# Head convolution of a decoder: symmetric pairs, their causal convolution and the sum over them, redistributed over four engines

## Reference, cut to what matters

```
kv = jnp.einsum('bhil,bhjl->bijhl', k_, v_)
kv_f = jnp.fft.rfft(kv, n=fft_size)
kernel_f = jnp.fft.rfft(ssm_kernel, n=fft_size)
y = jnp.fft.irfft(kv_f * kernel_f, n=fft_size)[..., :L]
out = y + kv * D[None, None, None, :, None]
out = jnp.einsum('bijhl,bhil->bjhl', out, q_)
```

## Time and profile before

| | us |
|---|---|
| median of 3 runs (1696.04 to 1698.32) | 1698.15 |
| the profiled execution: its own time | 1701.08 |
| its span in the trace | 1699.4 |
| PE / DVE / ACT / POOL busy | 1492.0 / 1142.3 / 672.0 / 712.8 |

### The profile page before, as it was taken

How to read it: one execution, slowest core, us unless ns; L and a number is a source line. 1 busy time by engine, 2 the same in 40 slices (tenths; PEclk the granted TensorE clock), 3 DMA queues, 4 the chain that set the end, 5 groups by cost and what they waited for, 6 DMA issues and landing times. The chain is left out here.

```text
span 1699.4 us, 34312 instructions
## 1 busy us (share of the span) xinstructions
PE 1492.0 (88%) x8665; PEld 1189.4 (70%) x8666; DVE 1142.3 (67%) x3594; ACT 672.0 (40%) x1818; POOL 712.8 (42%) x1162
## 2 busy tenths in 40 slices
PE   5899999999999999779897899876761999999997
PEld 4788888888888888566665666656760776677765
DVE  4777777777777777669999999997654223223232
ACT  3777777777767777610000100001331223332232
POOL 2011111111111110158887288861767355545553
PEclk9999999999999999999999899995555999999999
DMA  5544434343434343641113011104896455555552
GB/s 163 130 109 108 101 98 101 90 108 87 107 82 103 90 105 88 233 154 49 43 49 137 17 46 49 43 18 155 191 248 131 80 102 95 97 99 100 99 100 47
DMA packets 89774, 172.21 MB, mean 101 GB/s; under 512 B 26384, under 2 KB 26384, under 8 KB 88656
## 3 DMA queue, kind: packets, MB, share of 16 engines
q1 hardware_dynamic: 63584, 122.46, 27.3%
q0 software_dynamic: 18176, 35.80, 11.8%
q10 hardware_dynamic: 7920, 12.93, 3.0%
HBM read 78.10 MB, written 44.79 MB: 72 GB/s over the span
## 5 line engine op out<-in xcount | busy, mean ns | idle before, releaser
L1097 PE MATMUL ps_y<-pairs,taps 128*128 128x288 f32 x1280 | 324.5, 410 | 35.4 <-DVE prods L1170 32.1
L1097 PEld LDWEIGHTS ps_y<-pairs,taps 128*128 128x128 f32 x1280 | 238.6, 190 | 120.8 <-POOL pairs L1041 41.6
L853 ACT ACTIVATE probs<-neg_scores,neg_max 128x256 f32<-128x256 f32 x512 | 255.2, 505 | 25.9 <-DVE neg_max L654 25.9
L1170 DVE TENSOR_TENSOR prods<-ps_y,q_g 128x224 f32<-128x224 f32 (+7 forms) x960 | 251.4, 404 | 17.7 <-issue 8.0
L654 DVE CUSTOM_DVE_ANT_0 neg_scores<-ps_scores,alibi 128x256 f32<-128x256 f32 x512 | 194.9, 418 | 90.4 <-PE ps_scores L519 61.9
L1041 POOL TENSOR_TENSOR pairs<-ctx_g 128x32 f32 (+11 forms) x512 | 215.7, 459 | 42.4 <-PE ps_y L1097 32.0
L1533 POOL DMA_INDIRECT out<-y_row,back x72 | 113.2, 1572 | 174.9 <-DMA out<-y_row,back 140.6
L863 ACT ACTIVATE probs_t<-ps_probs_t 128x512 f32<-128x512 f32 x208 | 124.0, 596 | 130.4 <-PE ps_probs_t L530 130.4
L530 PE MATMUL ps_probs_t<-ident,probs 128*128 128x128 f32 x1024 | 159.3, 280 | 8.7 <-ACT probs L853 8.7
L403 POOL COPY inv_wide<-inv_sum 128x512 f32<-128x512 f32 x32 | 20.6, 672 | 318.7 <-DVE inv_sum L670 318.7
L1920 DVE TENSOR_TENSOR st_lo<-ps_x,st_hi 128x512 fp32r<-128x512 f32 x72 | 49.8, 692 | 145.8 <-ACT st_hi L1711 145.8
(11 more groups left out here) (190 smaller groups left out, 3232.6 us busy)
## 6 DMA issues: line engine op xcount, KB each, us to landing
q_stack<-q_hi SPq DMA_DIRECT2D x128, 128.0 KB, 2.3
k_stack<-k_hi SPq DMA_DIRECT2D x128, 128.0 KB, 2.3
taps<-kernel_pad SPq DMA_DIRECT2D x64, 256.0 KB, 3.1
x_in<-in_x SPq DMA_DIRECT2D x16, 512.0 KB, 3.6
q_stack<-q_lo SPq DMA_DIRECT2D x64, 128.0 KB, 2.3
k_stack<-k_lo SPq DMA_DIRECT2D x64, 128.0 KB, 2.3
x_rows<-x_mid SPq DMA_DIRECT2D x16, 512.0 KB, 3.0
ctx_g<-in_ctx_t SPq DMA_DIRECT2D x2, 4096.0 KB, 12.2
```

What stands on the lines that cost most here:

```text
L853: last = act.activation(probs[h % 2][:, tt, :], neg_scores[h % 2][:, tt, :], ACT.Exp, bias=neg_max[par][:, h, tt:tt + 1], scale=-1.0, accu ...
L1097: last = pe.matmul(ps_y[par][:, lc, 0:GB * PAIRS], taps[r][:, block_cols:block_cols + P], pairs[par][:, mc, :, :], start=(mc == 0), stop=( ...
L1170: last = dve.tensor_tensor(prods[par][:, :, :, to:to + n, term], y[:, :, :, col:col + n], head_of(q_g, own, q_from, n), ALU.mult)
```

## The change

- ACT gets work: for each head it copies q (`turn_q`) and ctx (`turn_ctx`) twice in a row into rings of 16 (`q_ring`, `ctx_ring`), so that a row of 8 read from element e on is the cyclic turn by e. It also copies y out of PSUM (`keep_y`, three instructions) into rows of 11 (`y_rows`), laid out so that each of the 8 terms is a plain row of 8.
- `form_pairs` is two multiplications in place of eight: one of 1024 elements (own channels repeated, times the ring) and one of 128. `pairs` has four buffers, and the pairs are formed three heads ahead.
- `multiply` is four multiplications in place of fifteen: one of 32 x 5 x 8 = 1280 elements and three of 256. It reads `y_rows` and `q_ring`, both in SBUF, and writes `prods` with the channel innermost. The elements are 2048, as before.
- The eight terms are summed by `halve` (1024 elements) and `quarter` (512) on DVE and `fold` (256) on POOL, which writes `q_g` and counts `z_ready`. The reduction is gone.
- PE waits for `y_kept` of the head two before, no longer for `prods_ready`, and writes each batch's 36 columns 64 apart in PSUM.
- Queues: DVE multiply(h), quarter(h-1), halve(h). POOL fold(h-1), form_pairs(h+3). ACT turn_q(h), keep_y(h), turn_ctx(h+3). The loops are unrolled by four heads.

```diff
-                    pool.wait_ge(y_ready, k * 2 + (g * SH + par + 1 - 2 + Y_START))
-                    for col, i, j, n in pair_segments():
-                        last = pool.tensor_tensor(pairs[par][:, :, :, col:col + n], ...)
-                    first = prods[par][:, :, :, :, 0:FOLD]
-                    pool.tensor_tensor(first, first, prods[par][:, :, :, :, SD - FOLD:SD], ALU.add).then_inc(folded, 1)
+                def form_pairs(g, k, r):
+                    h = k * PAIR_BUFS + (g * SH + r)
+                    pool.wait_ge(y_ready, h + (1 - PAIR_BUFS + Y_START))
+                    wait_apart(pool, ctx_ring_ready, h + 1, passed)
+                    own = by_lane(ctx_g, k * PAIR_BUFS + r)
+                    to = pairs[r][:, :, :, :].rearrange("p m b q -> p (m b) q")
+                    pool.tensor_tensor(to[:, :, 0:HALF * SD].rearrange("p n (d i) -> p n d i", i=SD),
+                                       own.unsqueeze(2).to_broadcast([P, EC * GB, HALF, SD]),
+                                       turned(ctx_ring[r % 2], HALF), ALU.mult)
+                    pool.tensor_tensor(to[:, :, HALF * SD:PAIRS], own[:, :, 0:HALF], own[:, :, HALF:SD], ALU.mult)\
+                        .then_inc(pairs_ready, 1)
+                def fold(g, k, r):
+                    wait_apart(pool, quartered, k * PAIR_BUFS + (g * SH + r + 1), passed)
+                    pool.tensor_tensor(by_lane(q_g, k * PAIR_BUFS + r), prods[r % 2][:, :, 0, :], prods[r % 2][:, :, 1, :],
+                                       ALU.add).then_inc(z_ready, 1)
...
-                    pe.wait_ge(prods_ready, h + (1 - 2 + PRODS_START))
+                    pe.wait_ge(y_kept, h + (1 - 2 + KEPT_START))
...
+                def turn_ctx(g, k, r):
+                    if not (is_int(k, 0) and r < 2 and g == 0):
+                        act.wait_ge(pairs_ready, k * PAIR_BUFS + (g * SH + r - 1))
+                    ring_of(ctx_ring[r % 2], ctx_g, k * PAIR_BUFS + r).then_inc(ctx_ring_ready, 1)
+                def turn_q(g, k, r):
+                    act.wait_ge(prods_ready, k * PAIR_BUFS + (r + g * SH + 1 - 2 + PRODS_START))
+                    ring_of(q_ring[r % 2], q_g, k * PAIR_BUFS + r)
+                def keep_y(g, k, r):
+                    act.wait_ge(y_ready, k * PAIR_BUFS + (r + g * SH + 1 + Y_START))
+                    ...
+                    act.activation(whole_rows[:, :, :, 0:SD], near, ACT.Copy)
+                    act.activation(whole_rows[:, :, 0:HALF - 1, SD:ROW], near[:, :, 1:HALF, SD - HALF + 1:SD], ACT.Copy)
+                    act.activation(rows[:, :, HALF * ROW:ROWS].rearrange("p n (u i) -> p n u i", u=2), ..., ACT.Copy).then_inc(y_kept, 1)
...
-                        for to, q_from, term in uses:
-                            last = dve.tensor_tensor(prods[par][:, :, :, to:to + n, term], y[:, :, :, col:col + n],
-                                                     head_of(q_g, own, q_from, n), ALU.mult)
-                    dve.tensor_reduce(head_of(q_g, k * 2 + par, 0, SD), prods[par][:, :, :, :, 0:SD - FOLD], AX_X,
-                                      ALU.add).then_inc(z_ready, 1)
+                    dve.wait_ge(y_kept, h + (1 + KEPT_START))
+                    dve.wait_ge(z_ready, h + (1 - 2 + Z_START))
+                    to, rows, q = prods[r % 2], y_rows[r % 2], q_ring[r % 2]
+                    dve.tensor_tensor(to[:, :, 0:HALF + 1, :], main_rows(rows, HALF + 1), turned(q, HALF + 1), ALU.mult)
+                    for e in range(HALF + 1, SD):
+                        first = (SD - e) * (ROW - 1)
+                        last = dve.tensor_tensor(to[:, :, e, :], rows[:, :, first:first + SD], q[:, :, e:e + SD], ALU.mult)
+                    last.then_inc(prods_ready, 1)
+                def halve(g, k, r):
+                    wait_apart(dve, prods_ready, k * PAIR_BUFS + (r + g * SH + 1 + PRODS_START), passed)
+                    dve.tensor_tensor(to[:, :, 0:4, :], to[:, :, 0:4, :], to[:, :, 4:8, :], ALU.add).then_inc(halved, 1)
+                def quarter(g, k, r):
+                    wait_apart(dve, halved, k * PAIR_BUFS + (r + g * SH + 1), passed)
+                    dve.tensor_tensor(to[:, :, 0:2, :], to[:, :, 0:2, :], to[:, :, 2:4, :], ALU.add).then_inc(quartered, 1)
```

More of the change, by code:

```diff
@@ L961, in build_decoder @@
         TAP_BUFS = 4
[L962 to L969, removed]
+        PAIR_BUFS = 4
+        PAIRS_AHEAD = 3
+        HALF = SD // 2
+        ROW = SD + HALF - 1
+        ROWS = HALF * ROW + SD
         with ExitStack() as scope:
@@ L980, in build_decoder @@
             taps = [sb(f"taps{i}", [P, E]) for i in range(TAP_BUFS)]
-            pairs = [sb(f"pairs{i}", [P, EC, GB, PAIRS]) for i in range(2)]
-            prods = [sb(f"prods{i}", [P, EC, GB, SD, SD]) for i in range(2)]
+            pairs = [sb(f"pairs{i}", [P, EC, GB, PAIRS]) for i in range(PAIR_BUFS)]
+            prods = [sb(f"prods{i}", [P, EC * GB, SD, SD]) for i in range(2)]
+            y_rows = [sb(f"y_rows{i}", [P, EC * GB, ROWS]) for i in range(2)]
+            q_ring = [sb(f"q_ring{i}", [P, EC * GB, 2 * SD]) for i in range(2)]
+            ctx_ring = [sb(f"ctx_ring{i}", [P, EC * GB, 2 * SD]) for i in range(2)]
             xn_g = [sb(f"xn_g{i}", [P, TT, E]) for i in range(2)]
@@ L1013, in head_of, with by_lane, turned, main_rows @@
                 return v.rearrange("p m b s i -> p m b (s i)")
+            def by_lane(tile, h):
+                v = tile[:, :, :].rearrange("p m (b s i) -> p (m b) s i", b=GB, s=SH)[:, :, ds(h, 1), :]
+                return v.rearrange("p n s i -> p n (s i)")
+            def turned(tile, n):
+                return bass.AP(tensor=tile, offset=0, ap=[[EC * GB * 2 * SD, P], [2 * SD, EC * GB], [1, n], [1, SD]])
+            def main_rows(tile, n):
+                return bass.AP(tensor=tile, offset=0, ap=[[EC * GB * ROWS, P], [ROWS, EC * GB], [ROW, n], [1, SD]])
+            def quads(eng, emit):
+                for r in range(PAIR_BUFS):
+                    emit(0, r)
+                with eng.Fori(1, QUADS - 1) as k:
+                    for r in range(PAIR_BUFS):
+                        emit(k, r)
+                for r in range(PAIR_BUFS):
+                    emit(QUADS - 1, r)
+            def head_at(k, r, ahead=0):
+                return k + (r + ahead) // PAIR_BUFS, (r + ahead) % PAIR_BUFS
+            def is_int(k, value):
+                return isinstance(k, int) and k == value
             skewed = bass.AP(tensor=kernel_pad, offset=1, ap=[[P + E, SH], [1, P], [1, E]])
@@ L1059, in _ @@
                                         newton[:, GT:NT], c_rstd_step, 0, c_rstd, passed)
[L1060 to L1065, removed]
+                    quads(pool, lambda k, r: head_step(g, k, r))
+                    fold(g, QUADS - 1, PAIR_BUFS - 1)
                 pool.wait_ge(x2_moments, GT)
@@ new lines, in quarter, with head_step @@
+                def quarter(g, k, r):
+                    wait_apart(dve, halved, k * PAIR_BUFS + (r + g * SH + 1), passed)
+                    to = prods[r % 2]
+                    dve.tensor_tensor(to[:, :, 0:2, :], to[:, :, 0:2, :], to[:, :, 2:4, :], ALU.add).then_inc(quartered, 1)
+                def head_step(g, k, r):
+                    multiply(g, k, r)
+                    if not (is_int(k, 0) and r == 0):
+                        quarter(g, *head_at(k, r, -1))
+                    halve(g, k, r)
@@ L1197, in _ @@
                     dve.wait_ge(c_xt_kept, (g + 1) * GB + XT_START)
[L1198 to L1206, removed]
+                    quads(dve, lambda k, r: head_step(g, k, r))
+                    quarter(g, QUADS - 1, PAIR_BUFS - 1)
                     for t in range(GT):
```

69 lines of the change are left out of this document (41 added, 28 removed).

## The result

The changed kernel takes 1786.68 us (median of 4 runs, 1783.06 to 1791.85), the kernel before 1698.24 beside it: a ratio of 1.0526, 95% interval 1.0496 to 1.0556. It is 88 us slower. Forecast were 1727 us and a range up to 1785, so the direction held, the forecast size was a third of the true one, and the time lies just outside the range.

The account below looks back on a forecast made before the run. DVE was taken to bound the kernel before; afterwards DVE and POOL times add. Group 0 +14.4, group 1 +13.3 and normalising +1 made +28.7 on 1701.08, 1729.8, set to 1727 us as that execution lay 2.9 above median; range 1700 to 1785.

Parts of the forecast that it names:

- DVE sets the pace before, PE next: Heads of the kernel before: DVE never stops at 5.64 us a head; PE needs 5.09 and waits 0.55.
- DVE and POOL shut each other out, so their times add: Changed heads: two-SBUF-input DVE instructions and POOL's SBUF reads exclude each other, so 3.74 + 2.41 = 6.15 us a head.
- I take 1.67 (same operation, tile and rows of eight): POOL's 1024-element pairs product: 1.67 us, from 1.375 ns an element in smaller products; 2.36 kept as upper end.
- second rival: Heads: exclusion plus dearer instructions, such as POOL's large product at 2.36 us, adding 40 us; 1745 to 1790 us, chance 28%.
- DVE alone 3.74: DVE's six instructions a head: 4.64 us at the plain rate, less 0.15 hidden for each, gives 3.74 instead of 5.64.
- the spread write alone made an element cost 1.9 ns: DVE's fifteen old multiplications: 1.9 ns an element against plain 1.057, the difference laid to writing eight words apart.
- the 0.25 us a head set beside the sum for rows that start on an odd word: DVE's new multiplications: odd-starting rows of eight at 1.30 ns an element would add 0.25 us a head, some 16 us.
- 0.1 us a head for handing over: Heads: waits between DVE and POOL where neither is ready, estimated at 0.1 us a head, between none and 0.3.
- The first rows of POOL beside the normalising, 1 us: Ahead of group 0: DVE's normalising beside POOL's first, longer pairs instructions adds 1 us (0 to 2).
- The first rival, PE sets the pace: Heads: no exclusion, PE at 4.97 us a head sets the pace; 43.5 us saved, 1655 us, chance 10%.
- The third rival: DVE's rows of eight stay at 1.9 ns an element, 1922 us; a lower TensorE clock shares its 5% chance.
- ACT's copies and PSUM columns 64 apart cost nothing: Heads: ACT's 3.0 us lies under PE's 5.09, only 1.8 us a group in the chain; spaced columns cost PE nothing.

Follow-up runs that it names:

- Pairs ahead: The kernel before with only pairs in four buffers, formed three heads ahead: 1700.61 us against 1700.02, ratio 1.0006.
- pool_writes_only: The changed kernel with POOL's 1024-element product replaced by writes of constants, so part of the computation is missing: 1665.9 us against 1692.45 for the kernel before.
- y_from_psum: The changed kernel with y multiplied straight from PSUM in nine instructions, without ACT's copies of y: 1672.15 us, ratio 0.988 to the kernel before.
- pool_probe: The changed kernel with six more POOL instructions of various sizes, operations and rows behind the last fold: 1787.41 us against 1692.45 for the kernel before.
- after_eight_products: The changed kernel with pairs formed by the eight short products of the kernel before: 1783.7 us against 1695.23 for the kernel before.
- psum_four_prods: The changed kernel with y multiplied from PSUM in nine instructions, no y copies, and four prods buffers instead of two: 1650.16 us, ratio 0.9724 to the kernel before.

## Why the prediction was right on the sign and wrong on the size

*DVE sets the pace before, PE next*: held. Pairs ahead, which touch neither, changed nothing.

*DVE and POOL shut each other out, so their times add*: held, and it makes the loss of the heads: with POOL's large product or DVE's multiplication taken out of it, the same kernel is faster than the one before. Shown from POOL's side by pool_writes_only and from DVE's by y_from_psum. The head of 7.18 us is the sum of what each holds, 4.03 + 3.14.

*The step that failed* is "I take 1.67 (same operation, tile and rows of eight)" for POOL's large product. It measured 2.29, with 2.25 between ends where the prediction's sum had 1.52. The other row of its size, 2364 ns, was a subtraction in one run and was set aside as another operation; pool_probe shows that size decides and operation and rows don't. The forecast had this case in its second rival (1745 to 1790, 28%), where the result fell, and the range ended 2 us short of it. The mechanism was right; this term of the sum was mis-sized. The term: 58 heads x 0.73 = 42 us.

*DVE alone 3.74*: it measured 4.03. The large multiplication came in as forecast (1.50 and 1.35 between ends). But what an instruction hides behind the one before, taken as 0.15 from the short ones, was 0.08 for `quarter` (0.68 long, 0.60 between ends) and `halve` (1.21 and 1.13), and the three short ones took 0.95 in place of 0.79. The term: 64 x 0.29 = 19 us. That the spread write alone made an element cost 1.9 ns was wrong as a reason: it was 0.8 of the 3.92 us. The rate taken for the new rows was right, and the 0.25 us a head set beside the sum for rows that start on an odd word did not come (1280 elements in 1.49 us).

*0.1 us a head for handing over*: there was none; -6 us.

*The first rows of POOL beside the normalising, 1 us*: it was 5.1. In the changed kernel the first product of PE comes 19.4 us after DVE's first normalising, before 14.3. DVE's normalisings, 0.55 us by themselves, stand behind POOL's products of 2.5 us:

```profile
731.70 9.60 DVE L1233 TENSOR_SCALAR xn_g<-x_res,all_moments,all_rstd 128x512 f32 x7 [2.72 <-PEq L1114]
731.86 2.51 POOL L1079 TENSOR_TENSOR pairs<-ctx_g,ctx_ring 128x1024 f32<-128x1024 f32 x1 [12.13 <-ACT ctx_ring L1169]
```

With eight short products (after_eight_products) it is 15.7, with constants written in place of the large products (pool_writes_only) still 18.9: here writing is in the way too, unlike in the heads, and a normalising stood up to 2.32 us. PE's transposes were slower as well, with a granted clock of 0.57 from 729 to 745 us where it was 0.79 before, so the 5.1 us are not all exclusion, and no run parts the two. The term: 4 us. The stage of attention ended 1.2 later in this execution.

Together 28.7 + 42 + 19 - 6 + 4 + 1 = 89 of the 90.7 us. Two terms are in neither sum and nearly cancel: PE's first head of group 0 took 1.6 us longer before DVE could start (its clock, below), and group 1 began 2.3 us sooner behind group 0, for a reason not looked for. So some 3 us are not accounted for.

*The first rival, PE sets the pace*: its price was 43.5 us saved. Against the kernel before, pool_writes_only saved 27 us and y_from_psum 20, and only psum_four_prods, without DVE's wait for `fold`, 48. It needed 0.45 us a head beside each other; there was none. *The third rival*: rows as dear as now are excluded by the 1.49 us, and the clock is told of below.

*ACT's copies and PSUM columns 64 apart cost nothing*: held. ACT is busy 89 of 215 us, and PE takes 4.85 us a head in psum_four_prods with the same columns.

## What to carry to other kernels

Before moving an operand of DVE from PSUM to SBUF, look what POOL reads meanwhile: if both DVE inputs are then in SBUF, add the two engines' times, don't take the larger. If they must meet, let POOL's long instruction start together with DVE's work from PSUM; an instruction of POOL that must follow DVE's sums, placed ahead of the long one, did that here (4.85 and 5.22 us a head with it, 6.5 to 7.0 without). For an instruction of a size that the trace has in one form only, price it by that size, not by a slope from smaller ones.

## What the runs showed of the hardware that was not expected

POOL's two-input instructions cost 2.2 to 2.4 ns an element from 256 elements on (0.61, 1.21, 2.30 us for 256, 512, 1024), the same for product and sum, in rows of eight or in one run. Two sums were somewhat dearer: `fold` at 0.72 us for 256, and the sum of 512 in the attention stage at 1.28.

POOL's writes of constants don't hold up a DVE multiplication with two SBUF inputs (1.49 us in all 64). DVE's normalising, with one tensor from SBUF and its output there, was held up beside them: 0.55 us by itself, up to 2.32 in pool_writes_only.

TensorE's granted clock was 0.94 and 0.95 over the heads of the changed kernel, while PE idled about 2 us in most of them, and 0.98 in psum_four_prods, where it was busy 156 of 163 us; both means lie near the upper of its two levels (2.4 and 1.2 GHz). The heads that PE ran at the lower level took it 6.8 us in place of 5.1, still less than the 7.18 of a head, so there the path did not run through it. At the start of group 0 it did: the granted clock was 0.76 from 751 to 758 us, PE's first head took 6.8 us (5.2 before), and DVE waited for it.
